# Cross attention: row maxima taken over two PSUM banks by one reduction

## The reference

```python
def _mha(x, ctx, mask, qw, qb, kw, kb, vw, vb):
    q = _split_heads(x @ qw + qb)
    k = _split_heads(ctx @ kw + kb)
    v = _split_heads(ctx @ vw + vb)
    scores = jnp.einsum('bqhd,bkhd->bhqk', q, k) / np.sqrt(D // H).astype(np.float32)
    if mask is not None:
        scores = scores + mask
    probs = jax.nn.softmax(scores, axis=-1)
    out = jnp.einsum('bhqk,bkhd->bqhd', probs, v)
    return out.reshape(x.shape[0], x.shape[1], D)
```

## Time and profile before

| what | us |
|---|---|
| median of 3 runs (lowest, highest) | 1320.55 (1318.86, 1325.93) |
| span of the profiled execution, first to last instruction | 1324.9 |
| busy of the span: PE, DVE, ACT, POOL | 1104.3, 1018.2, 869.6, 403.8 |
| first and last reduction of a grain (start) | 248.4, 880.2 |

### The profile page before, as it was taken

How to read it: one execution, slowest core, us unless ns; L and a number is a source line. 1 busy time by engine, 2 the same in 40 slices (tenths; PEclk the granted TensorE clock), 3 DMA queues, 4 the chain that set the end, 5 groups by cost and what they waited for, 6 DMA issues and landing times. The chain is left out here.

```text
span 1324.9 us, 33276 instructions
## 1 busy us (share of the span) xinstructions
PE 1104.3 (83%) x12028; PEld 602.7 (45%) x12028; DVE 1018.2 (77%) x2779; ACT 869.6 (66%) x1764; POOL 403.8 (30%) x832
## 2 busy tenths in 40 slices
PE   5799995699999999999999999986688878178894
PEld 2344443244444444444444444433344436167773
DVE  7488857588889898898988889956699968755554
ACT  3488873187887878788788787882488744233443
POOL 3211113223050320405023040021624227545552
PEclk9699997699999999999999999997799989588997
DMA  6970005513232132311323113002740022111113
GB/s 164 213 144 30 2 2 138 133 56 84 67 82 68 39 93 84 72 57 34 101 78 81 49 30 85 21 2 58 149 87 2 2 96 72 56 29 39 39 37 111
DMA packets 76648, 92.31 MB, mean 70 GB/s; under 512 B 8463, under 2 KB 62711, under 8 KB 76488
## 3 DMA queue, kind: packets, MB, share of 16 engines
q1 hardware_dynamic: 72392, 83.90, 25.1%
q0 software_dynamic: 2496, 5.12, 1.5%
q10 hardware_dynamic: 1600, 1.18, 0.3%
HBM read 64.37 MB, written 27.02 MB: 69 GB/s over the span
## 5 line engine op out<-in xcount | busy, mean ns | idle before, releaser
L1436 DVE TENSOR_REDUCE MG<-bank 128x1 f32<-128x401 f32 (+1 forms) x1024 | 515.4, 566 | 75.3 <-PE bank L1220 73.6
L1356 ACT ACTIVATE PT<-bank 128x512 f32<-128x512 f32 (+1 forms) x624 | 334.6, 597 | 64.3 <-PE bank L1238 63.8
L1238 PE MATMUL bank<-QP,KP 54*128 54x256 bf16 (+1 forms) x1664 | 252.4, 274 | 16.3 <-DVE CAT L1451 4.1
L1220 PE MATMUL bank<-KP,QP 54*128 54x401 bf16 (+1 forms) x1024 | 237.0, 344 | 14.8 <-DMA KP<-ctx_k_parts 9.6
L1258 PE MATMUL bank<-PT,VP 128*9 128x256 f32 (+1 forms) x2688 | 197.3, 367 | 0.8 <-ACT XT L1356 0.8
L1511 POOL TENSOR_TENSOR MP<-MN,ZERO 128x4 bf16<-128x4 f32 x128 | 26.4, 206 | 440.8 <-DVE MN L1443 435.8
L1238 PEld LDWEIGHTS bank<-QP,KP 54*128 54x128 bf16 (+1 forms) x1664 | 110.4, 96 | 108.3 <-ACT PT L1356 24.4
L1220 PEld LDWEIGHTS bank<-KP,QP 54*128 54x128 bf16 x1024 | 75.5, 94 | 125.0 <-DVE MG L1436 94.4
L1356 ACT ACTIVATE XT<-bank 128x512 f32<-128x512 f32 (+1 forms) x208 | 116.2, 599 | 20.3 <-PE bank L1238 19.9
L896 PE MATMUL bank<-QP,KP 51*128 51x256 bf16 x512 | 95.7, 281 | 33.6 <-ACT QP L827 8.8
L1258 PEld LDWEIGHTS bank<-PT,VP 128*9 128x9 f32 (+1 forms) x2688 | 76.0, 90 | 57.6 <-issue 20.4
(11 more groups left out here) (281 smaller groups left out, 2007.5 us busy)
## 6 DMA issues: line engine op xcount, KB each, us to landing
KP<-ctx_k_parts SPq DMA_DIRECT2D x128, 100.1 KB
ctx_k_parts<-KPARTS SPq DMA_DIRECT2D x16, 600.4 KB
KP<-ctx_k_parts SPq DMA_DIRECT2D x128, 59.4 KB
CN<-in_ctx SPq DMA_DIRECT2D x8, 768.0 KB
RAW<-in_w_gate_up SPq DMA_DIRECT2D x8, 512.0 KB, 3.8
QP<-q_parts SPq DMA_DIRECT2D x20, 192.0 KB
ctx_k_parts<-KPARTS SPq DMA_DIRECT2D x16, 200.1 KB
UQ<-bias_table SPq DMA_DIRECT2D x4, 768.0 KB, 8.5
```

The costliest lines, as they stand in the source:

```text
L1220: nc.tensor.matmul(GRAIN[n % NG][:, 0:w], k.QP[half, p, b * S + 128 * qt:b * S + 128 * (qt + 1)], k.KP[half, p, a:a + w], start=True, stop ...
L1238: return nc.tensor.matmul(bank[0:rows[t], S * at:S * (at + 1)], k.KP[half, p, 128 * t:128 * t + rows[t]], k.QP[half, p, b * S:(b + 1) * S] ...
L1356: nc.scalar.activation(PT[n % NP][0:rows[t], :], bank_of("s", g, t)[0:rows[t], :], ACT.Exp).then_inc(exp_done, 1)
L1436: nc.vector.tensor_reduce(MG[:, g % 4, 2 * s + qt, chunk:chunk + 1], GRAIN[n % NG][:, 0:w], AX.X, ALU.max).then_inc(m_read, 1)
```

## The change

A grain becomes two matmuls of one head and one query tile, into two neighbouring banks, and one reduction reads both banks. There are 8 grains per unit, of 400 + 400 or 401 + 401 keys, and the four banks are two pairs that take turns: a grain waits until the one two places earlier has been reduced. PSUM is declared as one tensor, so that one access pattern can cover two banks; `BANK` are slices of it at the same places. `MG` has two columns in place of four. In `cross_plan` the grains of a step stand right behind its scores, ahead of "h", the rounds and the bursts; `grain_order` no longer changes the half after each grain.

```diff
-    k.BANK = [k.stack.enter_context(nc.psum_tensor(f"bank{i}", [128, 512], F32)) for i in range(8)]
-    k.RING = [bank[:, :] for bank in k.BANK]
+    k.PSUM = k.stack.enter_context(nc.psum_tensor("bank", [128, 8 * 512], F32))
+    k.BANK = [k.PSUM[:, 512 * i:512 * (i + 1)] for i in range(8)]
+    k.RING = k.BANK
...
-    T, G, LEAD = NTILES, 16, 3
+    T, G, LEAD = NTILES, 8, 3
...
         plan.append(("s", t % T, t // T))
+        plan += [("g", g, 2) for g in range(G * j // T, G * (j + 1) // T)]
         if t % T == T - 2:
             plan.append(("h", T - 1, t // T))
...
-        plan += [("g", g, 2) for g in range(G * (j + 1) // T if j else 0, min(G, G * (j + 2) // T))]
...
-    rest = [[(s, qt, u, a, w) for qt in range(QT) for u, (a, w) in enumerate(chunks)] for s in range(2)]
+    rest = [[(s, qt, side) for qt in range(QT) for side in range(2)] for s in range(2)]
...
             order.append((rest[half] or rest[1 - half]).pop(0))
-            half = 1 - half
...
+    SIDES = [((0, 400), (400, 400)), ((800, 401), (1200, 401))]
...
-    NG = len(GRAIN)
+    NG = len(GRAIN) // 2
...
                 if n >= NG:
                     pe.wait_ge(m_read, n - NG + 1)
...
-                nc.tensor.matmul(GRAIN[n % NG][:, 0:w], k.QP[half, p, b * S + 128 * qt:b * S + 128 * (qt + 1)],
-                                 k.KP[half, p, a:a + w], start=True, stop=True).then_inc(m_ready, 1)
+                for i, (a, w) in enumerate(SIDES[side]):
+                    last = nc.tensor.matmul(GRAIN[2 * (n % NG) + i][:, 0:w],
+                                            k.QP[half, p, b * S + 128 * qt:b * S + 128 * (qt + 1)],
+                                            k.KP[half, p, a:a + w], start=True, stop=True)
+                last.then_inc(m_ready, 1)
...
-                nc.vector.tensor_reduce(MG[:, g % 4, 2 * s + qt, chunk:chunk + 1], GRAIN[n % NG][:, 0:w],
-                                        AX.X, ALU.max).then_inc(m_read, 1)
+                both = k.PSUM[:, 1024 * (n % NG):1024 * (n % NG + 1)].rearrange("p (i n) -> p i n", i=2)
+                nc.vector.tensor_reduce(MG[:, g % 4, 2 * s + qt, side:side + 1], both[:, :, 0:w],
+                                        AX.XY, ALU.max).then_inc(m_read, 1)
```

More of the change, by code:

```diff
@@ L1080, in cross_plan, with grain_order @@
             plan.append(("v", bursts[j], 0))
-        plan += [("g", g, 2) for g in range(G * (j + 1) // T if j else 0, min(G, G * (j + 2) // T))]
     return plan + [("o", 0, 0), ("neg", 0, 2), ("split", 0, 2)]
-def grain_order(chunks):
-    rest = [[(s, qt, u, a, w) for qt in range(QT) for u, (a, w) in enumerate(chunks)] for s in range(2)]
+def grain_order():
+    rest = [[(s, qt, side) for qt in range(QT) for side in range(2)] for s in range(2)]
     order, half = [], 0
@@ L1124, in phase_cross @@
     nc = k.nc
-    T, N, G = NTILES, NCTX, 16
+    T, N, G = NTILES, NCTX, 8
     rows = [min(128, N - 128 * t) for t in range(T)]
@@ L1129, in phase_cross @@
     chunks = [(c * CW, min(CW, N - c * CW)) for c in range(4)]
-    grains = grain_order(chunks)
+    grains = grain_order()
+    SIDES = [((0, 400), (400, 400)), ((800, 401), (1200, 401))]
     NV = len(V_BURSTS)
@@ L1151, in phase_cross @@
         OT = k.sb("OT", [128, NO, S], stack=st)
-        MG = k.sb("MG", [128, 4, 4, 4], stack=st)
+        MG = k.sb("MG", [128, 4, 4, 2], stack=st)
         MN = k.sb("MN", [128, 4, 4], stack=st)
@@ L1208, in grain @@
                 b, p = batch_of(g)
-                s, qt, _, a, w = grains[u]
+                s, qt, side = grains[u]
                 half = slice(HALF * s, HALF * s + CROSS_ROWS)
@@ L1431, in maxima @@
                 n = G * g + u
-                s, qt, chunk, a, w = grains[u]
+                s, qt, side = grains[u]
+                w = SIDES[side][0][1]
                 if u == 0 and g >= 4:
```

## The result

The changed kernel takes 1349.97 us (median of 4 runs, 1347.32 to 1352.83), the kernel before 1320.49 on the same chip: a ratio of 1.0211, 95% interval 1.0174 to 1.0247.

A forecast was written before the change was run, and what follows sets the result against it. A TensorE and ScalarE chain was taken to bound the kernel, VectorE counting in 1.53 of a plain unit's 8.78 us. Seven batches +24.0, the last batch +3.3, grain-only units -0.9: +26.4 on 1320.55 gives 1347 us, range 1322 to 1366.

The forecast's parts named there:

- The reduction: On VectorE, one reduction of 802 elements takes about 0.99 us, 0.91 from start to start, against 0.96 for two old ones.
- The head: Plain unit's start to the end of its second burst of values: 5.23 us, before 5.28, a gain of 0.05.
- The tail: Plain unit from second burst's end to next unit: 4.15 us, before 3.50; the last grain waits 1.90 in place of 1.53.
- Plain units: Units without rounds go from 8.78 to 9.37 us, that is +0.59.
- Units with rounds: Pairs 1 to 5 of a batch, +0.39 us each, because TensorE itself is late behind the second burst.
- pair 0: A batch's unit that stands still for the division, then goes on like a unit with a round: +0.3 us.
- the last tile: Behind the second burst, its halves and the grain between: next grain after 0.82 us, 0.35 plus a wait of 0.47.
- VectorE as the bound: Rival: VectorE's saved 0.4 us counts in each of some 61 units, -26 us, 1294 us, at least 1312; chance 0.13.
- No change: Rival: three-bank ring and ScalarE's 7.51 us set the pace and hide the added wait; about 1320 us, chance 0.07.
- only plain units: Rival: rounds give VectorE and TensorE enough else to do, so +10 us, 1331; inside the forecast's 0.78 chance.
- A reduction as dear as two: Rival: the two-bank pattern costs 0.96 and 1.13 us, 0.19 more per unit, 12 in all, 1359; inside the forecast's 0.78.
- The clock: Rival: TensorE's granted clock falls from 1.00 as its pauses grow about 0.6 us a unit; over 1500 us, chance 0.02.

The follow-up runs named there:

- The narrow reductions: Changed kernel with each reduction over only the first 100 columns of both banks: 1329.45 us, ratio 1.0070.
- the run with two reductions: Changed kernel, each pair reduced by two one-bank instructions and given back when the second ends: 1357.61 us, ratio 1.0263.
- the grains in their old places: Changed kernel with the grains back where they stood in the list before, behind the bursts and ahead of the next scores: 1363.15 us, ratio 1.0348.
- new places: Kernel before, single-bank grains and four turns kept, with the grains moved right behind the scores: 1310.79 us, ratio 0.9917.
- matmuls two by two: Changed kernel's order, but each bank reduced, handed over and given back by itself, four banks in turn: 1350.2 us, ratio 1.0186.

## Why the prediction was right

Its steps, in its order. *The reduction*: 0.99 and 0.91 forecast, 0.984 to 0.990 and 0.90 measured. *The head*: 5.23 forecast, 5.24; the grain of two matmuls ahead of the first burst put this burst at 589.33, 1.53 after the start (1.51 forecast). *The tail*: 0.55, 1.90, 0.06, 0.43 and 1.21 forecast; 0.56, 1.89, 0.05, 0.45 and 1.20 measured. Plain units 9.37 and 9.39. The narrow reductions show that TensorE's wait for VectorE in the tail is the cause there: without it 8.56.

*Units with rounds*: +0.39 forecast for each of pairs 1 to 5; +0.38 to +0.40 for pairs 1 to 4, +0.55 for pair 5, and +0.11 for pair 0 where 0.3 stood. These two terms were mis-sized and nearly cancel: a batch lost 3.46 where 3.43 was forecast, closer than its parts. That TensorE itself is late in the tail of the unit with keys shows in its timeline:

```profile
541.84 0.28 PE L1240 MATMUL bank<-QP,KP 54*128 54x256 bf16 x1
...
542.20 0.62 PE L1240 MATMUL bank<-QP,KP 54*65 54x256 bf16 x2
542.53 0.51 PE L1220 MATMUL bank<-KP,QP 54*128 54x401 bf16 x2
...
543.19 0.94 PE L1293 MATMUL bank<-CT,WQK 128*128 128x401 f32 x2
544.07 0.40 PE L1240 MATMUL bank<-QP,KP 54*128 54x256 bf16 x4
544.29 0.84 PE L1220 MATMUL bank<-KP,QP 54*128 54x400 bf16 x4
545.07 1.05 PE L1260 MATMUL bank<-PT,VP 128*9 128x256 f32 x16
```

Scores and then four matmuls of one half run behind the round without a wait, and the burst begins 3.23 behind the second burst's end at 541.84, where 3.33 was forecast (0.82 + 0.34 + 0.22 + 0.96 + 0.90, and 0.09 for the switch). The term that was too long is the last tile: the next grain came after 0.69 (542.53), not 0.82, because its wait was 0.33 here and not 0.47. And the head, which the prediction left as it was, grew by 0.12 (541.84 - 535.88 = 5.96, before 5.84). The tail of 4.43 (4.54 forecast) and this head make +0.40, so that +0.39 came so close is luck in part: two errors of about 0.12 cancel. The mechanism, TensorE late by itself, stands: the narrow reductions leave this unit at 10.39.

*The rivals.* VectorE as the bound: no; it gave up 0.5 us of work in a plain unit and the unit grew. No change and only plain units: no, every unit with grains grew, but for one that before had run at a granted clock of 0.87 (pair 0 of the seventh batch, 13.57 and then 12.29). A reduction as dear as two: 9.52, as the run with two reductions shows, and 9.39 was measured. The clock: 1.00 in every unit of the changed kernel behind the first, so it isn't the cause. That first unit, which the windows above leave out, ran at 0.62 and before at 0.73. The eleven units at 0.90 to 0.94 with the grains in their old places show that it can fall in units of this kind.

What the prediction didn't see is that its sum holds effects of opposite sign. The plain units show the shares, each row with one step more (us; the parts are the head, from there to VectorE's start, the reductions that the last grain waits for, to that last grain, and from it to the next unit; in the third row the last grain stands for its second matmul):

| plain unit | head | start | reductions waited for | last grain | to the next unit | sum |
|---|---|---|---|---|---|---|
| kernel before | 5.28 | 0.38 | three, 1.53 | 0.06 | 1.53 | 8.78 |
| new places | 5.12 | 0.46 | three, 1.53 | 0.07 | 1.47 | 8.65 |
| matmuls two by two | 5.24 | 0.46 | four, 2.01 | 0.07 | 1.47 | 9.25 |
| pair handed over and given back as a whole | 5.25 | 0.55 | four, 2.01 | 0.07 | 1.64 | 9.52 |
| one reduction over both: the changed kernel | 5.24 | 0.56 | two long, 1.89 | 0.05 | 1.65 | 9.39 |

The prediction laid the longer wait, 1.90 for 1.53, on the two turns. That reason was wrong: with four banks in turn and the same order it is 2.01, since eight matmuls stand behind the second burst where seven stood. What the whole pair costs as such is the 0.09 and the 0.17 of the fourth row. The order is the largest step, and the walk along the rows had its size only because it followed the new order, matmul by matmul.

## What to carry to other kernels

An instruction that handles two buffers at once also gets both late and gives both back late. Before fusing, follow the loop that sets the period through the timelines and count on which edge the fused work lies. Here, in a plain unit, the fused reduction gained 0.13 us, handing over and giving back both banks at once cost 0.27, and the order that the pairs brought with them cost 0.60. Where producer and consumer share few buffers, how many of the items stand behind the producer's long burst can matter as much as how long one takes: one pair moved ahead of the burst brought back 21 us here, and reductions of about a third of the length 20.5 (1349.97 to 1329.45).

## What the runs showed of the hardware

A reduction over two PSUM banks by one access pattern costs what its elements cost: 984 ns for 802 against 567 for 401, 1.04 ns an element, with nothing to be seen for the border between the banks; the narrow ones, 200 elements over two banks, took 366 ns, 1.00 ns less for each of the 201 elements that 401 of one bank are more. Reductions in a row overlap: they start 0.48 us apart where one takes 0.57, and 0.90 where one takes 0.99. Two matmuls of different halves of the partitions start 0.01 apart (590.31 and 590.32 in the timeline after), the two of one grain, in one half, 0.18 (590.32 and 590.50). So the half in which a grain stands counts: behind the round of the unit with keys, four matmuls of one half and the scores ahead of them take 1.00 to the burst (544.07 to 545.07), where with single grains in the new places scores and three grains took 0.67 (527.32 to 527.99). How much of this 0.33 is the half and how much the one matmul more, no run takes apart.
